# A decoder layer on one core: cross attention's first maxima made in self attention's last turns, setup work moved in time, and an expert block's two scatters issued together

## The reference, cut to what matters

```python
def xattn(query, key, value, ...):                    # B=32, T=112, S=375, 16 heads of 16
    q1, q2 = (q[..., :8], q[..., 8:])                 # 2 x 16 heads = 32 "units"
    k1, k2 = (k[..., :8], k[..., 8:])
    a1 = softmax(q1 @ k1.T * SCALING)
    a2 = softmax(q2 @ k2.T * SCALING)
    lam = exp(dot(lambda_q1, lambda_k1)) - exp(dot(lambda_q2, lambda_k2)) + LAMBDA_INIT
    return ((a1 - lam * a2) @ v) * (1 - LAMBDA_INIT) @ out_proj_weight.T + out_proj_bias

def ffn(x, gate_w, w1, w2, w3):                       # 8 experts, F=1024
    mult1, mult2, idx = sparse_mixer_top2(x @ gate_w.T)
    for e in range(8):
        w_tok = mult1 * (idx[:, 0] == e) + mult2 * (idx[:, 1] == e)
        out = out + w_tok[:, None] * ((silu(x @ w1[e].T) * (x @ w3[e].T)) @ w2[e].T)
    return out

x = layernorm(x + attn(x)); x = layernorm(x + xattn(x, ctx, ctx)); x = layernorm(x + ffn(x))
```

## Time and profile before

| what | value |
|---|---|
| device time, median of 3 runs | 1797.75 us (1795.05 to 1801.78) |
| the profiled execution: its time, its span | 1796.06 us, 1794.3 us |
| mean granted clock of PE | 0.955 |
| busy: PE, DVE, ACT, POOL | 1566.2, 1128.1, 900.5, 757.1 us |
| stages, from the first instruction | front to 438, cross to 1200, experts to 1765, finish to 1794 us |

### The profile page before, as it was taken

One profiled execution on the slowest core, in us unless ns is written; L12 is line 12 of the kernel. 1 busy time (PEld: TensorE's weight loads), 2 busy tenths in 40 slices (PEclk: granted clock), 3 DMA queues, 4 the chain that ended last, 5 costly groups with the idle time before them and its releaser, 6 DMA issues. The chain is left out here.

```text
span 1794.3 us, 46494 instructions
## 1 busy us (share of the span) xinstructions
PE 1566.2 (87%) x17664; PEld 1195.9 (67%) x17664; DVE 1128.1 (63%) x2617; ACT 900.5 (50%) x2175; POOL 757.1 (42%) x920
## 2 busy tenths in 40 slices
PE   4899999984999999999999999829999999999991
PEld 2677777763566666666666666518898898898891
DVE  4566666662888788778888888634444444444443
ACT  2344455442466666666666666604444443443444
POOL 6334444322755556765676567421121111121112
PEclk9999999997799999999999999959999999999996
DMA  6666776634455545554554455167776766766744
GB/s 178 180 188 187 194 195 186 193 113 99 136 139 142 149 138 136 164 153 136 141 161 145 134 154 153 49 224 250 245 267 215 245 228 228 246 216 229 260 143 173
DMA packets 205508, 318.92 MB, mean 178 GB/s; under 512 B 61000, under 2 KB 174056, under 8 KB 205288
## 3 DMA queue, kind: packets, MB, share of 16 engines
q1 hardware_dynamic: 183784, 249.78, 45.3%
q0 software_dynamic: 21504, 66.19, 12.6%
HBM read 224.52 MB, written 91.03 MB: 176 GB/s over the span
## 5 line engine op out<-in xcount | busy, mean ns | idle before, releaser
L1154 DVE TENSOR_REDUCE cross_mx<-cross_bank_max 112x2 f32<-112x750 f32 x512 | 460.2, 931 | 115.4 <-PE cross_bank_max L1273 113.1
L985 ACT ACTIVATE cross_probs<-cross_bank_score 125x448 f32<-125x448 f32 x768 | 406.2, 545 | 238.2 <-PE cross_bank_score L1263 235.4
L1461 POOL DMA_INDIRECT acc<-experts_y,experts_dest_i x64 | 100.0, 1562 | 459.4 <-DMA acc<-experts_y,experts_dest_i 260.6
L1263 PE MATMUL cross_bank_score<-cqst,ckst 97*125 97x448 f16 x768 | 282.7, 370 | 4.7 <-ACT cross_probs L985 2.4
L1273 PE MATMUL cross_bank_max<-ckst,cqst 96*112 96x375 f16 x1024 | 257.5, 334 | 28.8 <-DVE cross_mx L1154 21.1
L1538 DVE TENSOR_TENSOR experts_hid<-experts_bank_h,experts_gated 128x256 f32<-128x256 f32 (+1 forms) x288 | 113.4, 394 | 245.2 <-ACT experts_gated L1487 240.2
L1572 PE MATMUL experts_bank_h<-experts_x_hi,w 128*128 128x256 f16 (+1 forms) x1536 | 239.1, 267 | 22.3 <-DVE experts_hid L1538 20.9
L1289 PE MATMUL cross_bank_out<-cross_probs,cross_val 125*32 125x112 f32 x6144 | 201.6, 264 | 0.1
L1572 PE MATMUL experts_bank_h<-experts_x_lo,w 128*128 128x256 f16 (+1 forms) x768 | 198.9, 267 | 0.0
L1273 PEld LDWEIGHTS cross_bank_max<-ckst,cqst 96*112 96x112 f16 x1024 | 128.9, 133 | 89.1 <-DVE cross_mx L1154 36.3
L1487 ACT ACTIVATE experts_gated<-experts_bank_h 128x256 f32<-128x256 f32 (+1 forms) x288 | 103.1, 358 | 155.2 <-PE experts_bank_h L1572 152.5
(11 more groups left out here) (245 smaller groups left out, 3045.1 us busy)
## 6 DMA issues: line engine op xcount, KB each, us to landing
w<-w_halves SPq DMA_DIRECT2D x24, 3072.0 KB, 11.8
experts_w_third<-w_halves SPq DMA_DIRECT2D x12, 3072.0 KB, 11.7
cross_ew<-in_experts POOLq DMA_DIRECT2D x32, 768.0 KB, 5.6
w_halves<-cross_ew_half POOLq DMA_DIRECT2D x32, 768.0 KB
ckst<-cross_k SPq DMA_DIRECT2D x96, 187.5 KB
cross_v<-front_v SPq DMA_DIRECT2D x24, 531.2 KB
cross_val<-cross_v SPq DMA_DIRECT2D x32, 398.4 KB
front_src<-in_ctx_t SPq DMA_DIRECT2D x24, 500.0 KB, 6.0
```

Of the source, the lines that this page charges most:

```text
L985: nc.scalar.activation(probs[:, e % PROBS], bank_score[e % 2][0:SC, 0:4 * T], ACT.Exp, scale=CROSS_SCALE).then_inc(probs_ready, 1)
L1154: nc.vector.tensor_reduce(mx[:, b % nb, 2 * n:2 * n + 2], bank_max[n % 2][0:T, :, 0:S], AX.X, ALU.max).then_inc(max_read, 1)
L1263: nc.tensor.matmul(bank_score[e % 2][0:SC, 0:pair_w], kst[:, p, g, k * SC:(k + 1) * SC], qst[:, p, g, :], start=True, stop=True).then_inc( ...
```

## The change

1. Cross attention's maxima of batch 0 are made in front: `cross_units(c, e)` gives the units of a slot, 32 in all, five in each of turns 28 to 31 (two of them in slot 3) and four in each of turns 32 to 34. A unit is one matmul (96 x 112 by 375) and one reduction of 112 x 375, one unit for each instruction. Their stacks (`load_cross` 0 and 1) are loaded at the end of turns 22 and 24, not 32. The two transposes, the negated copies and the row's two DMAs follow in turns 32, 34, 35. Stage cross then begins with scores of batch 0 and maxima of batch 1 together.
2. `ident` is made once, in front. Lambda is worked out in slots 4, 5 and 6 of cross's turn 0.
3. The dummy's and `acc`'s paddings are written in turn 2. The eight region paddings are issued from two queues, SP's and ACT's. The rows of expert block 0 are loaded by SP at cross's end, behind the first padding and all scatters; experts begins with their transpose.
4. A block's scatters are both issued when block j-1's have landed. `destinations(j)` moves from f == 2 to f == 5.

```diff
+        def cross_units(c, e):
+            if B - 4 <= c < B:
+                at = 5 * (c - B + 4) + e
+                return (at, at + 1) if e == 3 else (at,)
+            at = 20 + 4 * (c - B) + e
+            return (at,) if c >= B and at < 2 * H else ()
...
+                def cross_row(h):
+                    wait(sp, cross_row_read, h + 1)
+                    wait(sp, early_loaded[0], 16 * 15)
+                    sp.dma_start(cqst[STACK:STACK + 1, 0, 4 * h:4 * h + 4, :].rearrange("o g (i t) -> o (g i) t", t=T),
+                                 neg_mx[:, h]).then_inc(cross_row_loaded, 16)
...
-                    if c == B:
+                    if c in (B - 10, B - 8):
+                        b = (c - B + 10) // 2
...
-                        for b in range(2):
-                            load_cross(sp, b, cross_k, cross_q, ckst, cqst, early_loaded)
+                        load_cross(sp, b, cross_k, cross_q, ckst, cqst, early_loaded[b])
+                    if c == B + 2:
+                        cross_row(0)
+                cross_row(1)
...
                         for j in groups_at(n, e):
                             evacuate(n, j)
+                        for u in cross_units(c, e):
+                            wait(dve, cross_max_full, u + 1)
+                            nc.vector.tensor_reduce(cross_mx[:, u:u + 1], bank_proj[u % 2][0:T, 0:S], AX.X, ALU.max).then_inc(cross_max_read, 1)
...
+                def cross_maximum(u):
+                    g, i = divmod(u, 4)
+                    if u == 0:
+                        wait(pe, early_loaded[0], 16 * 15)
+                    if u < 2:
+                        wait(pe, group_read, groups_before(ITEMS))
+                    wait(pe, cross_max_read, u - 1)
+                    nc.tensor.matmul(bank_proj[u % 2][0:T, 0:S], cqst[0:STACK, 0, g, i * T:(i + 1) * T], ckst[0:STACK, 0, g, :],
+                                     start=True, stop=True).then_inc(cross_max_full, 1)
...
                         for j in todo[1:]:
                             project(n, j)
+                        for u in cross_units(c, e):
+                            cross_maximum(u)
+                        if (c, e) in CROSS_ROWS:
+                            cross_rows(CROSS_ROWS.index((c, e)))
...
                 sp.wait_ge(pad_ready, 1)
-                sp.wait_ge(padding_ready, 4)
-                for e in range(EXP):
...
+                for e in range(0, EXP, 2):
+                    pad_region(sp, e, padded if e else pad_first)
+                sp.wait_ge(pad_first, 16)
+                sp.wait_ge(scattered, 32 * B)
+                sp.dma_start(first_rows[:, 0], routed[0:BLOCK, :].rearrange("(i p) n -> p i n", p=128)).then_inc(first_loaded, 16)
...
+                act.wait_ge(pad_ready, 1)
+                for e in range(1, EXP, 2):
+                    pad_region(act, e, padded)
...
             def _(dve):
-                dve.wait_ge(consts_loaded, 16 * consts)
...
-                        if k != 1 and on(c + lead):
+                        if (c, e) in (LAMBDA_AT[0], LAMBDA_AT[2]):
+                            difference(LAMBDA_AT.index((c, e)))
+                        if k != 1 and later(c + lead):
...
                 for j in range(BLOCKS):
                     p = j % 2
                     wait(pool, meta_done, j + 1)
+                    wait(pool, y_stored[1 - p], 16 * slot_tiles_before(j, 1 - p))
                     for i in range(tiles(j)):
                         wait(pool, y_ready, tiles_before(j) + i + 1)
-                        if i:
-                            wait(pool, y_stored[p], 16 * (slot_tiles_before(j, p) + i))
-                        else:
-                            wait(pool, y_stored[1 - p], 16 * slot_tiles_before(j, 1 - p))
...
-                        if f == 2:
-                            destinations(j)
                         if f == 4 and on(j + 1):
                             x_low(j + 1)
+                        if f == 5:
+                            destinations(j)
```

More of the change, by code:

```diff
@@ L704, in batches_to_scatter, with cross @@
     return None, ()
[L707 removed]
+def cross(nc, a, cross_k, cross_q, cross_v, x1, w_halves, routed, acc, rows, table_i, table_f, w, kst, qst, ident, first_rows):
     nb = CROSS_RING
@@ L712, in cross @@
     on = lambda b: 0 <= b < B
+    later = lambda b: 1 <= b < B
+    made = lambda name, b: b if name in ("row0", "row1") else b + 1
+    row_loads = lambda b: 16 * (b // nb + (1 if b % nb else 0))
     pair_w = 4 * T
@@ L837, in row @@
                     p = b % nb
-                    wait(sp, read[f"row{h}"], b + 1)
+                    wait(sp, read[f"row{h}"], made(f"row{h}", b))
                     sp.dma_start(qst[STACK:STACK + 1, p, 4 * h:4 * h + 4, :].rearrange("o g (i t) -> o (g i) t", t=T),
@@ L1300, in step @@
                         of = c + STEP_AT[before][1] + turn_back
-                        if on(of):
-                            wait(pe, read[before], of + 1)
+                        if on(of) and made(before, of):
+                            wait(pe, read[before], made(before, of))
                             break
```

156 lines of the change are left out of this document (84 added, 72 removed).

## The result

The changed kernel takes 1785.01 us (median of 5 runs, 1782.06 to 1789.41) against 1797.75 us before (median of 5 runs, 1795.05 to 1802.02): ratio 0.9927, 95% interval 0.991 to 0.9944. That is faster by 0.7%, a third of the gain that was forecast (1759, range 1742 to 1772), and outside the range. The profiled execution has a span of 1780.3 us against 1794.3, 14.0 us less.

A forecast was written before the change was run, and what follows sets the result against it. PE was taken to bound the large stages, with time also held in two seams and short experts stalls. 1796.06 - 2.4 - 6.3 - 28 - 1.5 = 1757.9 us, forecast as 1759 in terms of the median, range 1742 to 1772.

The forecast's parts named there:

- the 1.5 of the sum: End of experts: block 34's scatters issued together halve the last scatter's 3.08 us wait, gaining 1.5 us.
- Rival 3: Experts: stalls only shrink to PE's direct waits, gain 20.9 us, time 1766 or 1771; chance 0.1.
- rival 5: Experts: paired scatters slow the weight loads, 1816 us if each load takes 16 us; chance 0.02.
- Two queues issue four each: Cross to experts: eight paddings issued in 5.7 us, done at 1188.7; a step in the seam's 6.3 us gain.
- The last scatter's landing: Cross to experts: cross's last scatter lands between 1190.2 and 1195.1, taken as 1192; the rows' load waits for it.
- rival 4: Cross to experts: paddings from two queues bring nothing, since the DMA engines are the limit; 1766 us, chance 0.06.
- Scores need nothing more: Cross's start: only the first weighing waits, for `val`; it comes at 464.8, not 467.20, gaining 2.4 us.
- At turn 22 the row has more room, 0: Front: the early stack load at turn 22 delays no maxima row that PE needs; cost 0.
- 3.3 us for turn 24: Front: the stack load at turn 24 delays batch 26's row to 366.3, so PE stands 3.3 us.
- Val "right behind" lambda's loads: Cross's start: `val` follows lambda's loads on the queue and lands 8.2 us after the stage's start.
- the chain argument: Front's last turns are a chain, not a load, so the units inside it lengthen front by 14.4 us.
- Rival 2: Front: the units fit into gaps, front ends at 442.2, gain 16.8 in place of 2.4; 1744 us, chance 0.2.

The follow-up runs named there:

- e3: The changed kernel with a block's scatters again one after the other, destinations still after f == 5; 1787.72 us, ratio 0.9932.
- e10: The changed kernel without part 1, with destinations back after f == 2 and scatters side by side; ratio 0.9773.
- e11: The changed kernel without part 1, with all eight region paddings issued from SP's queue; ratio 0.9793.
- e4: The changed kernel with POOL's splitting of expert weights one turn later in its program; 1776.31 us, ratio 0.9867.
- e7: The changed kernel with `val` of batch 0 loaded as cross's first DMA; 1787.17 us, ratio 0.9922.
- e8: The changed kernel with four repairs: stack loads later, units in gaps, `val` first, POOL's splitting one turn later; 1756.57 us, ratio 0.9752.
- e13: The kernel with all four repairs, POOL also holding two 768 KB transfers until batch 1's maxima row has landed; 1754.39 us, ratio 0.9749.
- e5: The changed kernel with cross's early stack loads at the end of front's turns 26 and 30, not 22 and 24; 1776.49 us, ratio 0.9855.
- e6: The changed kernel with front's units moved to slots 1 and 2, one in slot 3 in turns 28 to 31; 1780.70 us, ratio 0.9898.
- e9: The changed kernel without part 1, with lambda's instructions back at the start of cross's programs; 1841.51 us, ratio 0.9862.
- e15: The kernel with all four repairs, run again on one chip with e13 and e14; 1762.06 us, ratio 0.9778.
- e14: The changed kernel without part 1, run again on one chip with e13 and e15; 1753.62 us, ratio 0.9744.
- e1: The changed kernel without part 1, batch 0's maxima made in cross again; 1755.72 us, ratio 0.9757.
- e2: The changed kernel with part 4 undone: scatters one after the other, destinations after f == 2; 1816.88 us, ratio 1.01.

## Why the prediction was wrong

**Part 4, experts: right.** 27.5 us from the transposes to the end, forecast 29.5. The mechanism (DVE at the destinations for the second scatter of j-2) was right, and the prediction did not ask whether both halves are needed: each gives the whole gain alone (e3, e10). The small blocks' loss was 0.48 us each, not 0.3. Behind the last weight load the change gained 0.5 us, not the 1.5 of the sum. Rival 3 and the slower rival 5 fall: weight loads landed in 12.1 and 12.4 us (11.8 before), far from 15.5.

**Part 3, second seam: right in size, wrong in cause.** 5.4 us against 6.3. That the size came out is luck. "Two queues issue four each" was the step that carried it, and e11 shows it is worth 0.6 us at most. The last scatter's landing, 7.7 us, was the long bound and not the middle I took. The Trainium skill ("DMA: Bandwidth & Descriptors", section "Issuing engines are not separate DMA queues"), which I weighed and set aside, says that issuing from several engines saves only sequencer time, usually small beside the DMA. The runs bear this out in what reached PE: the second queue cut the issuing from 11.3 to 6.3 us, but the paddings landed later and PE began 0.6 us earlier at most. So rival 4 had the queues right, and yet its 1766 did not follow, since the seam gained by the edits that e11 keeps.

**Parts 1 and 2: wrong, by 21.3 of the 24 us that the sum was off.** The table's stretches split this into four steps, 12.9 + 7.4 + 4.1 - 3.1:

1. "Scores need nothing more": the sentence on cross's start asked only what the first weighing needs, and took the rest of cross as unchanged. It was 12.9 us longer. Turn -1 held not only maxima; it was the cover under which POOL split one part of the weights and began the second ahead of PE's scores. With it gone, POOL's small steps for batch 0 began 9.6 us after `mv` was ready, PE stood 7.5 us and then ran 8 us at the half clock (e4, e7). Undoing this gave 5.1 us (e4). For the rest the record has candidates, the late row of batch 1 and the clock behind it (e8, e13), but no run that accounts for it. No rival named POOL: I had read POOL's prelude as work that goes.
2. "At turn 22 the row has more room, 0", and 3.3 us for turn 24: together 10.7 in place of 3.3. The load at turn 22 cost 1.9 us, that at turn 24 a wait of 5.85, and behind it the clock fell for some 6 us, which was in no term (e5). The row was issued at 364.87, not at 361.6: six loads of stacks took 3.85 us behind the fifteen new DMAs, 2.74 before.
3. Val "right behind" lambda's loads: it landed 12.3 us after the stage's start, not 8.2. The four lambda loads took 3.45 us to issue, not 1.88, and `val` stands behind them. The first weighing thus came 4.1 us later than forecast. Repairing it alone gave no time, since POOL came later still (e7).
4. The units: forecast 14.4, with the tail's 0.3 14.7, measured 11.6 up to the stage's end (22.3 less 10.7). Here the chain argument was right, and it was shown by moving them: from turn 28 to 34 the units cost 1.8 us in the gaps in place of 10.6 (e6). Rival 2 was thus possible, but not with the order of this change.

**Part 2**, priced at nothing, gives 6.8 us where part 1 is left out (e9); what it does in the whole change no run tests. In the kernel before and in e9 DVE stands at the head of cross for lambda's loads, in front of the work that sets the stage's start.

**What stays open.** With all repairs cross is still longer from the first weighing to the first padding than without maxima in front: 721.9 us in e13, 719.7 in e15 against 713.7 in e14. Single falls of the clock and a wait of 1.5 us for ACT's `rows` in e13 may be part of it; no run took them apart. Nor is it known why the same row lands in 6 us in one execution and in 9 in another. Profiles of the same kernel differ there by 3 us (e1 and e14: 716.7 and 713.7), and those of the change, e2 and e3, alike up to that point, by 6, so part of this distance is within what single traces can tell.

## What to carry to other kernels

When a stretch is taken out of a stage, list what every other engine did in it, not only the engine that set its length: the work that was hidden beside it now stands in the open, and an engine whose program is unchanged can become the late one. A small DMA on the critical path is priced by what stands ahead of it on its queue at that moment: the same fifteen DMAs cost 8.3 us less four and six turns later (e5). Price each part alone before the whole: here the parts without the largest one were 29 us faster than all together.

## What the runs showed of the hardware

Two indirect scatters issued 1.85 us apart had both landed 8.80 us after the second's issue had ended, one alone took 7.80. Over the stage POOL waited 8.9 us in the mean for a pair (e10, 62.6 us in 7 waits) and 7.6 us for one (e3, 265.2 us in 35).

Eight paddings of 260 KB were issued in 11.3 us from one queue and landed 3.4 us after issue in the median (e11); from two queues they were issued in 6.0 us and landed after 6.0 us (ACT's) and 6.7 us (SP's; the change). What was saved at the issue was in part spent on the way.

A maxima row of 3.5 KB landed in the median 4.9 us after its issue in front and 3.8 us in cross (before); in e8's cross 2.2 us. Between the same two transfers of 768 KB one such row took 9.2 us in e8 and 6.2 us in e15.

PE's waits cost more than their length where the granted clock fell behind them from 2.4 to 1.2 GHz. In the change it stood at 0.50 from 371 to 376 behind the wait of 5.85 us, at 0.58 from 493 to 497 behind that of 2.35, and at 0.50 from 522 to 530 behind that of 7.50; in e8 at 0.50 from 476 to 481 behind that of 4.07. The length of the wait alone does not tell it: behind the wait of 1.94 us the clock stayed at 1.00 from 340.5 to 350, and behind one of 1.52 us in e13 it stood at 0.57 from 492 to 500.
